# Running an image's experts in its own pipeline period: 50 row scatters in one burst

## The reference

```python
x = x + _L0_conv_ref(_ln_c(x), L0_conv_W)                  # all-pairs similarity
t = t + _L0_ffn_ref(_ln_t(t), gate_w, gate_b, w1, w2, w3)  # 16 experts, top 2
x = x + _L1_conv_ref(_ln_c(x), offset_w, offset_b, dcn_w)  # deformable 3 x 3
t = t + _L1_ffn_ref(_ln_t(t), wr, br, w1, b1, w2, b2)      # FFN on the routed half
```

## Time and profile before

| | |
|---|---|
| median of 3 runs | 4388.02 us (4370.83 to 4394.26) |
| the profiled execution's own time | 4384.43 us |
| its span, first to last instruction | 4382.6 us |
| busy: PE, DVE, ACT, POOL | 66%, 55%, 40%, 65% |

### The profile page before, as it was taken

One profiled execution on the slowest core, in us unless ns is written; L12 is line 12 of the kernel. 1 busy time (PEld: TensorE's weight loads), 2 busy tenths in 40 slices (PEclk: granted clock), 3 DMA queues, 4 the chain that ended last, 5 costly groups with the idle time before them and its releaser, 6 DMA issues.

```text
span 4382.6 us, 51090 instructions
## 1 busy us (share of the span) xinstructions
PE 2905.4 (66%) x17558; PEld 1877.7 (43%) x17558; DVE 2431.0 (55%) x3753; ACT 1773.7 (40%) x2917; POOL 2846.7 (65%) x2608
## 2 busy tenths in 40 slices
PE   5969678577847886768778776778671357156432
PEld 2424533453446335633465345634560247135321
DVE  6453444754575556655675566655653345346775
ACT  5657456235523652356424552456221112122210
POOL 0040073777777776777767777777777777776760
PEclk8979688568856885679666886689665556565555
DMA  5000214331433142523342244314441334243546
GB/s 124 8 15 1 47 25 91 95 92 40 124 99 111 38 110 80 131 59 98 86 115 79 55 114 112 106 40 111 109 113 40 110 104 116 60 126 90 123 113 118
DMA packets 540584, 375.70 MB, mean 86 GB/s; under 512 B 465712, under 2 KB 470576, under 8 KB 540336
## 3 DMA queue, kind: packets, MB, share of 16 engines
q0 software_dynamic: 110848, 257.07, 20.2%
q1 hardware_dynamic: 429488, 115.37, 12.5%
HBM read 308.76 MB, written 89.41 MB: 91 GB/s over the span
## 4 chain that ended last, share of the span: by engine, by line
POOL 42%; PE 23%; issue 14%; DVE 11%; ACT 4%; DMA 3%; DVEq 2%; SPq 1%; ACTq 0%; POOLq 0%
POOL G L540 27%; PE PS L1683 22%; POOL shared L554 9%; POOL slot_rows L546 6%; DVE G L615 2%; DMA G<-corner_table,index 1%; DVE G L621 1%; DMA out<-experts_w 1%; DVEq L617 1%; DVE st L582 1%; DVE small L971 1%; PE PS L1721 1%; DVE values L623 1%; ACT small L1545 0%; DVE smallc L582 0%
## 5 line engine op out<-in xcount | busy, mean ns | idle before, releaser
L540 POOL DMA_INDIRECT G<-corner_table,index x1800 | 1999.6, 1111 | 716.8 <-issue 535.6
L615 DVE TENSOR_TENSOR G<-G,corner_w 128x768 f32<-128x768 f32 x600 | 541.5, 953 | 640.7 <-DMA G<-corner_table,index 640.7
L1522 ACT ACTIVATE work<-work 128x768 f32<-128x768 f32 (+2 forms) x800 | 667.1, 853 | 358.6 <-DVE work L948 250.3
L1683 PE MATMUL PS<-xn 128*128 128x400 f16 (+3 forms) x3200 | 657.6, 347 | 220.2 <-DVE work L948 208.7
L948 DVE TENSOR_SCALAR work<-PS 128x768 f32<-128x768 f32 (+2 forms) x496 | 474.6, 971 | 490.2 <-ACT work L1522 329.6
L546 POOL DMA_INDIRECT slot_rows<-split_a,slot x400 | 451.4, 1129 | 334.0 <-DVE slot L1045 212.3
L1683 PE MATMUL PS<-work,xm 128*64 128x400 f32 (+3 forms) x3200 | 631.9, 516 | 0.0
L554 POOL DMA_INDIRECT shared<-slot_results,slot x400 | 394.6, 986 | 352.0 <-DMA slot_results<-shared 230.4
L1683 PEld LDWEIGHTS PS<-xn 128*128 128x128 f16 (+1 forms) x3200 | 281.5, 101 | 667.7 <-DVE work L948 319.8
L1721 PE MATMUL PS<-ident,values 128*128 128x128 f32 x800 | 184.8, 375 | 496.9 <-DVE xq L628 251.7
L1683 PE MATMUL PS<-dcn,val_cm 128*128 128x64 f32 x2000 | 418.0, 362 | 59.4 <-ACT val_cm L1425 59.4
(11 more groups left out here) (259 smaller groups left out, 3357.8 us busy)
## 6 DMA issues: line engine op xcount, KB each, us to landing
G<-corner_table,index POOLq DMA_INDIRECT x1800
corner_table<-rows_scratch SPq DMA_DIRECT2D x32, 784.0 KB
shared<-slot_rows SPq DMA_DIRECT2D x32, 512.0 KB, 7.5
slot_results<-shared SPq DMA_DIRECT2D x32, 512.0 KB
corner_table<-G SPq DMA_DIRECT2D x8, 841.0 KB, 10.4
slot_rows<-split_a,slot POOLq DMA_INDIRECT x400
shared<-slot_results,slot POOLq DMA_INDIRECT x400, 2.4
experts_w<-x_scratch SPq DMA_DIRECT2D x8, 784.0 KB, 6.3
```

Of the source, the lines that this page charges most:

```text
L540: GP.indirect_dma_start(G[0:rows, n % 2, tap * 4 * C:(tap + 1) * 4 * C], None, tables[b % 2], bass.IndirectOffsetOnAxis(ap=index[0:rows, c ...
L615: V.tensor_tensor(g, g, bc(w, 2, C), ALU.mult)
L1522: A.activation(sq[0:rows, u % 4, :, 0:n], relu[0:rows, u % 2, :, 0:n], ACT.Square).then_inc(s["squared"], 1)
L1683: return P.matmul(o, a, b, start=start, stop=stop, skip_group_check=True)
```

## The change

The experts of image u move from unit u+1 into unit u, and all that follows them moves one unit earlier with them: in every place where an older image is named, u-1 becomes u, u-2 becomes u-1, and so on. `UNITS` becomes B + 1 = 9, so one unit falls away.

```diff
-A_TURN, ..., MOE_TURN, STAT_TURN, STACK_TURN = 2, 3, 5, 3, 6, 5, 7, 16, 16
+A_TURN, ..., MOE_TURN, STAT_TURN, STACK_TURN = 2, 3, 5, 3, 6, 5, 8, 16, 17
-SCATTERS_FIRST, SCATTERS_PER_TILE = 26, 4
+SCATTER_TILE, SCATTERS_PER_TILE = 4, 50
...
-        UNITS = B + 2
+        UNITS = B + 1
...
         def scatters_after(t):
-            return range(SCATTERS_FIRST + (t - LATE) * SCATTERS_PER_TILE,
-                         min(SCATTERS_FIRST + (t - LATE + 1) * SCATTERS_PER_TILE, 2 * T))
+            first = (t - SCATTER_TILE) * SCATTERS_PER_TILE
+            return range(first, min(first + SCATTERS_PER_TILE, 2 * T)) if first >= 0 else ()
...
+            def scatter_first(i, n):
+                if n == 0:
+                    pool.wait_ge(s["slots_ready"], i + 1)
+                scatter_rows(i, n)
...
             def unit(u):
+                if valid(u - 1):
+                    gather_results(u - 1)
                 if valid(u - 2):
-                    gather_results(u - 2)
+                    for t in range(LATE, T):
+                        gather_tile(u - 2, t)
+                if not valid(u - 1):
+                    for n in range(2 * T):
+                        scatter_first(u, n)
                 if valid(u - 1):
-                    pool.wait_ge(s["slots_ready"], u)
-                    for n in range(SCATTERS_FIRST if valid(u - 3) else 2 * T):
-                        scatter_rows(u - 1, n)
-                if valid(u - 3):
-                    for t in range(LATE, T):
-                        gather_tile(u - 3, t)
-                        if valid(u - 1):
+                    for t in range(LATE if u - 1 < LAST else T):
+                        gather_tile(u - 1, t)
+                        if valid(u):
                             for n in scatters_after(t):
-                                scatter_rows(u - 1, n)
-                if valid(u - 2):
-                    for t in range(LATE if u - 2 < LAST else T):
-                        gather_tile(u - 2, t)
+                                scatter_first(u, n)
```

More of the change, by code:

```diff
@@ L334, in turn_weigh @@
             first = T - LATE - len(LATE_WEIGH)
-            return (u - 3, T - first + r) if r < first else (u - 2, r - first)
+            return (u - 2, T - first + r) if r < first else (u - 1, r - first)
         def turn_sample(u, r):
             first = T - FIRST - len(LATE_SAMPLE)
-            return (u - 3, T - first + r) if r < first else (u - 2, r - first)
+            return (u - 2, T - first + r) if r < first else (u - 1, r - first)
         def turn_holds(u, b):
-            return valid(b) and (u < B + 1 or b < LAST)
+            return valid(b) and (u < B or b < LAST)
         def turns(u):
-            return SLOTS if u < B + 1 else TAIL_SLOTS
+            return SLOTS if u < B else TAIL_SLOTS
         def moe_steps(r):
@@ L358, in stack_turn @@
         def stack_turn(r):
-            i = r - STACK_TURN
-            return (5 * i, min(5 * i + 5, 2 * NCH)) if i >= 0 else (0, 0)
+            return (0, 2 * NCH) if r == STACK_TURN else (0, 0)
         def ffn_chunks(r):
@@ L469, in unit @@
             def unit(u):
[L470 to L473 removed]
+                if valid(u - 3):
+                    store_x3(u - 3)
+                if valid(u - 1):
+                    write_table(u - 1)
                 if u + 1 < B:
@@ L911, in beside_mixer @@
                 for step in range(3):
[L912 to L921, removed]
+                    if valid(k - 1) and (j, u) == (4, 3 * step):
+                        combine(k - 1, step)
+                    if valid(k - 1) and (j, u) == (5, 3 * step):
+                        geo_start(k - 1, step)
+                if valid(k - 1):
+                    geo_prepare(k - 1, j - 7, u)
+                if valid(k - 3):
+                    ffn_prepare(k - 3, j, u)
+                if valid(k - 2) and j in LATE_SAMPLE and u == MIX_ADD:
+                    sample_add(k - 2, late_sample(j))
                 for piece in range(5):
-                    if valid(k - 3) and j in LATE_WEIGH and MIX_WEIGH[piece] == u:
-                        weigh(k - 3, late_weigh(j), piece)
+                    if valid(k - 2) and j in LATE_WEIGH and MIX_WEIGH[piece] == u:
+                        weigh(k - 2, late_weigh(j), piece)
             def idle_mixer(k):
@@ L1124, in turn @@
                 for i in range(4):
[L1125 to L1128, removed]
+                    if valid(k - 3) and r == FFN_TURN + 1 + i:
+                        ffn_bias(k - 3, i)
+                if valid(k - 3) and r == FFN_TURN + 4:
+                    ffn_weigh(k - 3)
                 for step in range(2):
-                    if valid(k - 2) and r == GEO_TURN + step:
-                        geo_second(k - 2, step)
+                    if valid(k - 1) and r == GEO_TURN + step:
+                        geo_second(k - 1, step)
                 for n in norm_pieces(r):
@@ L1135, in turn @@
                 for g in moe_steps(r):
-                    if valid(k - 1) and 1 <= g <= GROUPS:
-                        hidden(k - 1, g - 1)
+                    if valid(k) and 1 <= g <= GROUPS:
+                        hidden(k, g - 1)
                 for step in range(2):
-                    if valid(k - 3) and r == STAT_TURN + step:
-                        ffn_stat(k - 3, step)
+                    if valid(k - 2) and r == STAT_TURN + step:
+                        ffn_stat(k - 2, step)
             def unit(k):
@@ L1492, in beside_mixer @@
             def beside_mixer(k, j, u):
[L1493 to L1498, removed]
+                if valid(k - 1) and (j, u) == (6, 1):
+                    ln_std("g", k - 1, 0)
+                if valid(k - 1):
+                    geo_prepare(k - 1, j - 7, u)
+                if valid(k - 3):
+                    ffn_prepare(k - 3, j, u)
                 for stage in range(2):
-                    if valid(k - 3) and j in LATE_SAMPLE and MIX_EVAC[stage] == u:
-                        sample_evac(k - 3, late_sample(j), stage)
+                    if valid(k - 2) and j in LATE_SAMPLE and MIX_EVAC[stage] == u:
+                        sample_evac(k - 2, late_sample(j), stage)
             def idle_mixer(k):
@@ L1540, in mixer @@
                     act.wait_ge(s["mixed"], 2 * (hn + 1) + g0 + SPH)
-                    if valid(k - 2) and 2 * (k - 2) + half > 0:
-                        act.wait_ge(s["geo_done"], 2 * (k - 2) + half)
+                    if valid(k - 1) and 2 * (k - 1) + half > 0:
+                        act.wait_ge(s["geo_done"], 2 * (k - 1) + half)
                     for blk in range(4):
@@ L1611, in turn @@
                 for c in ffn_chunks(r):
-                    if valid(k - 4):
-                        gelu_chunk(k - 4, c)
-                if valid(k - 1) and r == MOE_TURN:
+                    if valid(k - 3):
+                        gelu_chunk(k - 3, c)
+                if valid(k) and r == MOE_TURN:
                     A.activation(table_cell[:, 1:2], table_cell[:, 0:1], ACT.Silu)
@@ L1619, in turn @@
                 for g in moe_steps(r):
-                    if valid(k - 1):
-                        expert_step(k - 1, g)
-                if valid(k - 3) and r == STAT_TURN:
+                    if valid(k):
+                        expert_step(k, g)
+                if valid(k - 2) and r == STAT_TURN:
                     for q in range(4):
-                        square("f", k - 3, tmp, fc, q)
+                        square("f", k - 2, tmp, fc, q)
                 if k + 1 < B:
@@ L1812, in beside_mixer @@
             def beside_mixer(k, j, v):
[L1813 to L1816, removed]
+                if valid(k - 1):
+                    geo_prepare(k - 1, j - 7, v)
+                if valid(k - 3):
+                    ffn_prepare(k - 3, j, v)
                 for stage in range(3):
-                    if valid(k - 3) and j in LATE_SAMPLE and MIX_SAMPLE[stage] == v:
-                        sample(k - 3, late_sample(j), stage)
+                    if valid(k - 2) and j in LATE_SAMPLE and MIX_SAMPLE[stage] == v:
+                        sample(k - 2, late_sample(j), stage)
             def idle_mixer(k):
@@ L1860, in mixer @@
                         sims(1, 0, 1)
[L1861 to L1864, removed]
+                    if valid(k - 1) and half:
+                        pe.wait_ge(s["om_taken"], 2 * k)
+                    if valid(k - 3) and not half:
+                        pe.wait_ge(s["f_cm"], (k - 2) * NCH)
                     pe.wait_ge(s["z_ready"], k * 2 + half + 1)
@@ L1971, in turn @@
                 for c in ffn_chunks(r):
-                    if valid(k - 4):
+                    if valid(k - 3):
                         if c == 0:
-                            pe.wait_ge(s["f_cm"], (k - 3) * NCH)
-                            ffn_up(k - 4, 0)
+                            pe.wait_ge(s["f_cm"], (k - 2) * NCH)
+                            ffn_up(k - 3, 0)
```

(18 more changed lines are left out.)

20 lines of the change are left out of this document (10 added, 10 removed).

## The result

The changed kernel takes 4600.19 us (median of 4 runs, 4598.11 to 4603.57) against 4385.08 us (4 runs): a ratio of 1.0494, 95% interval 1.0464 to 1.0525. It is slower, as forecast, by 215 us where 267 were foretold (4655 against a median of 4388); the time lies inside the range.

What follows compares the result with a forecast made beforehand. POOL was taken to bound the kernel from the first result gathers to the last. Terms -150 + 68 + 5 x (68 - 12) + (15 + 56) = +269 us on 4384.4 gave 4653, stated as 4655, range 4550 to 4740.

Steps and rivals of the forecast that it cites:

- front, to image 0's result gathers: Start of the program: image 0's result gathers come in unit 1, at about 398 us; -150 us, bounds -145 to -157.
- first interval: Result gathers of image 0 to those of image 1: scatters now stand between tiles 4 and 5; +68 us.
- five full units: Each full unit: +68 us for the burst in the tail, -12 us in the mixer.
- last interval, now with a mixer: Image 6's result gathers to image 7's: +15 us for becoming a full unit, plus 56 for tail and mixer.
- behind image 7's result gathers: End of the program: the part keeps its order and its 630.9 us.
- What bounds the kernel: POOL is the bound from the first result gathers to the last: 453 us of work in full units of 467.4 us.
- The burst in the tail: Each full unit's tail: 50 scatters show whole, 64.7 us at 1.29 each, tail +68; dearer bound 74.4, tail +78.
- The mixer's gain: Second half of each full unit's mixer, freed of scatters: -12 us from 124, PE's 102.4 us needing 111; at most 28.
- The unit that fell away: Image 6's to image 7's result gathers: 452.5 us without mixer becomes a full unit of 467.4, +15 us, plus tail and mixer.
- the burst is not hidden: Rival for the tail: something other than POOL sets its pace, scatters cost nothing, -207 us, 4181 us; 6 in 100.
- The mixer was not held up by POOL alone: Rival: POOL alone held up the mixer, so its second half falls to unit 2's 96 us, total 4560; full gain 15 in 100.
- The experts were not starved: Rival: PE's lower clock after the gap makes experts' results late, 80 us more, 4735; with dear scatters 15 in 100.

Runs made afterwards that it cites:

- experiment 2: Changed kernel with the burst of 50 scatters behind the sixth sampled tile (tile 5), one tile later in POOL's program: 4552.95 us, 1.0372 of the kernel before.
- experiment 3: Changed kernel with the burst of scatters behind the fourth sampled tile (tile 3), one tile earlier: 4673.07 us, 1.0670 of the kernel before.
- experiment 4: Changed kernel with only the 25 first-choice scatters per image, waits for half the count, output not the reference's: 4348.46 us, 0.9934 of the kernel before.
- experiment 1: Changed kernel with scatters back in the next unit's mixer, experts reading rows scattered one image earlier, output not the reference's: 4243.02 us, 0.9686 of the kernel before.
- experiment 7: Changed kernel with the burst behind tile 5, two sampled tiles more in the mixer and two turns less in the tail: 4595.66 us, 1.0490 of the kernel before.

## Why the prediction was right, step by step

In us on the span; measured from the rows where result gathers begin:

| term | foretold | measured | how |
|---|---|---|---|
| front, to image 0's result gathers | -150 | -158.9 | 388.89 - 547.76 |
| first interval | +68 | +63.7 | (867.06 - 388.89) - 414.5 |
| five full units | 5 x 56 | 5 x 50.8 | (3457.91 - 867.06) / 5 = 518.2, less 467.4 |
| last interval, now with a mixer | +71 | +63.7 | (3974.05 - 3457.91) - 452.5 |
| behind image 7's result gathers | 0 | -3.3 | 627.6 - 630.9 |
| sum | +269 | +219 | 4601.7 - 4382.6 |

All five terms came out on the faster side (by 9, 4, 26, 7 and 3 us), so no error hid another.

*What bounds the kernel*: right, and shown by POOL's rows in experiments 2 and 3 and by the half burst of experiment 4; experiment 1 fits it. *The burst in the tail*: right in size. It was priced from unit 0 at 64.7 us and took 65.5; the dearer bound of 74.4 from the mixer does not apply. But the reason given with the price, DVE nearly idle in unit 0, was misread. The window over that burst, in the kernel before, columns as in the earlier trace rows:

```profile
252.00:317.00 65.00, 45.63 (x267) 20.60 (x268) 32.40 (x52) 45.42 (x65) 49.37 (x50) 0.82 0.08 25
```

DVE was busy for half of it. The price held because of what DVE did there: 17.0 of the 32.4 us are relu steps (L948) that read PSUM. If every scatter of the kernel before is paired with the DVE instructions that ran during it, the 75 that ran beside nothing but TENSOR_TENSOR with all inputs in SBUF took 1423 ns on the mean, the 68 beside such reads of PSUM alone 954, and the 108 beside nothing 969. So it was in part luck that the row chosen had the right price. Over the whole program the mean scatter fell from 1129 to 1004 ns. That and the pairing agree with the Trainium skill ("SBUF — State Buffer", Who interferes with whom), by which a DVE instruction with two SBUF inputs holds up GpSimd instructions that read SBUF. That an indirect DMA, whose indices lie in SBUF, counts as such a reader is what these rows suggest. The pairing is read from the trace; no experiment here varied DVE's work alone.

*The mixer's gain* is the term that was mis-sized: 124 to 108 us, a gain of 16 where 12 were foretold. PE's share of the time stayed what unit 2 had shown (99.43 of 108, 92%), as the working assumed. But the 102.4 us of PE work that I divided by it were not fixed: they fell to 99.4, and the granted clock of the window is 0.95 where it was 0.91. With tiles that come in time PE stood still less (8.6 us of the window, 21.6 before) and ran more of the half at the higher of its two clocks; that the one caused the other is read from the rows, not tried. Experiment 1, with its scatters back in the mixer, has 104.91 us and 0.90 again.

*The front* came 9 us earlier than foretold: the last scatter was issued at 318.8 and PE took the first sorted rows at 324.48, so landing and loading took under 6 us (1.2 to SP's first load at 320.00, 4.5 on to PE) and not the 14 that I had added up. The 12.0 us in that sum were taken from unit 6, where POOL's gathers ran beside the loads and PE had other work in its program; which of the two made them long is not shown. *The first and the last interval* fell short by 4 and 7 us; the last has the mixer's larger gain in it, the rest I cannot divide further. *The unit that fell away*: right, it brought only its front. POOL had been busy through it from end to end, and that work had to be done in any case.

The rivals: the burst is not hidden, since half of it gives back half. The mixer was not held up by POOL alone: it fell to 108 us, not to unit 2's 96. The experts were not starved: result gathers in the changed kernel still start 0.3 us behind the last sampling gather. That cover was thin, though, as experiment 7 showed when it took a turn away. Of the expected signs three were a little off: POOL's waiting is some 63 us a unit (53 in the mixer, 10 ahead of the burst), not 70; DVE waits 67.39 us for tile 5, not 55; image 1's result gathers start at 867, not at 880.

## What to carry to other kernels

Add an engine's issue gaps to its busy time before calling it idle: POOL at 65% had five units with 3% of slack. When a queue that works in order is the bound, shortening the pipeline removes only the stretches in which that queue waited; the work moves, and a unit "saved" is worth what was empty in it. And moving work on such a queue can cost twice, once where it goes (here some 65 us in the tail) and once where it leaves a hole that bounded buffers cannot fill (here 16 us came back in the mixer), so look for the hole's next tenant (a tile, a later burst) before making the move, and keep count of the cover it stands on.

## What the runs showed of the hardware

An indirect scatter of 128 rows took 1.28 us from start to start where DVE had next to nothing to do (experiment 3: 64.0 us for unit 5's burst, DVE busy 4.4 of them), 1.31 in the changed kernel, 1.40 with a second tile to weigh beside it (experiment 2: 70.0 us, DVE busy 24.6), and 1.49 in the mixer of the kernel before. One scatter of the changed kernel and the three weighing products that ran beside it:

```profile
2723.35 2.63 POOL L545 DMA_INDIRECT slot_rows<-split_a,slot  x1 [0.31 <-issue]
...
2722.47 2.67 DVE L618 TENSOR_TENSOR G<-G,corner_w 128x768 f32<-128x768 f32 x3
```

The sampling gathers became a little dearer (mean 1132 ns, 1111 before) with POOL's total nearly the same. The same pairing says where that comes from. Gathers beside nothing on DVE took 944 ns in both kernels, those beside TENSOR_TENSOR with all inputs in SBUF alone 1304 before and 1346 after. What POOL's instructions took above 0.95 us each fell from 72 to 22 us for the scatters and rose from 298 to 336 for the gathers: the scatters had left DVE's weighing, so more of its hold-ups fell on gathers. This too is read from overlaps in the traces, not tried.
